# P's pass without the low half of h in its first block of channels, and the diagonals on GpSimd

## The chip, the cores and the metric

One core of a Trainium2 chip runs the kernel. The metric is the time of one execution on the device in microseconds (us); smaller is better. The time given is the median of three runs.

## The reference

There are 128 graphs of 128 nodes with 512 channels each, one adjacency matrix of 128 x 128 for all, and two layers.

```python
h = relu(layernorm(x))
z_l = h @ W_lang.T;  z_g = h @ W_grav.T;  v = h @ W_V.T
zn  = z_l / max(norm(z_l), eps)
A_l = max(zn @ zn.T, 0) * not_eye                     # cosine similarities
d2  = max(sq + sq.T - 2 * z_g @ z_g.T, 0)             # sq: squared norms of z_g
A_g = exp(-d2 / (2 * sigma**2)) * not_eye
K   = w_l * row_normalised(A_l * adj) + (1 - w_l) * row_normalised(A_g * adj)
x   = x + (K @ v) @ W_O.T
h2  = relu(layernorm(x))
x   = x + (adj * adj).T @ h2 + bias
```

W_lang has been scaled up by 8. Everything is float32.

## The kernel before

**Form of the computation.** The kernel never forms z_l and z_g. It takes M = W.T W once (for each of the two, l = 0 and 1) and needs S = h M h.T. M is symmetric, so only its blocks on and below the diagonal are kept (`Lw`, the ten blocks of `TRI`, those on the diagonal halved). With y the product of this half and h, P = y h.T is half of the result, and S = P + P.T. The values are float32 split into two parts of a shorter type, hi and lo, and a product is three matmuls (`passes`): hi·hi, hi·lo, lo·hi. Low parts are made as value minus hi, the hi part on ScalarE, the subtraction mostly on VectorE.

**Tiling and loops.** 32 groups of four graphs each (`NG`, `GB`). Each engine has a program of its own with a loop over the groups (`iteration(i)`), written out by hand; within an engine the order is that of the code, and semaphores with counts tie engines together. Iterations 0, 1, the last but one and the last stand outside of the loop. PSUM has a ring of five banks: use n may start when `drained` says that use n - 5 has been emptied (`free`).

**One iteration i on TensorE** (from `iteration` in the tensor block): eight y blocks (four blocks of channels a, l = 0 and 1), 60 matmuls of 512 columns; P's pass (line 1109), for each a and each graph b three matmuls of 256 columns, 48 in all, into `p_ps`; v of the first graph, 12 matmuls; K·v of group i - 1, 12 matmuls (waits for `kt_split`); v of the other three graphs, 36; layer 1 of group i - 2, 12. The y blocks of the next iteration wait for all four `ht_lo`.

**P to S.** ScalarE copies P out of PSUM in two halves (line 530, `p_copied`). VectorE multiplies each half by `select`, a repeated mask `diag_of` that keeps two diagonals (line 900, `diagonal`), reduces them to squared norms (line 907, `squares`), and clips them (line 911). GpSimd raises them to the power -1/2 (line 404, `row_norms`). P is turned by a transpose in blocks on VectorE (line 878, `turn_p`, once for each l), a store to DRAM, and eight loads back in turned order on SyncE's queue (lines 251 and 256). In the next iteration VectorE adds P and its turned copy (line 884, `sum_s`), ScalarE takes the exponential, and mask, row sums and factors follow on VectorE. VectorE then forms K (line 730, `combine`, `k_ready`) and K is turned in the same way: transpose (line 737), a store (line 281), four loads (line 286), then the copy `KT_hi` (line 610) on ScalarE and the subtraction `KT_lo` (line 746, `kt_lo`, gives `kt_split`) on VectorE. The buffer of the diagonals also holds the blocked P and K on their way out.

**VectorE around the change**, in order: the eight `y_lo` (line 669) with the work on S and K between them, the block transposes of the next group's h (line 685), four `bn_stats` (line 680), first diagonal, `KT_lo`, squares, second diagonal, squares, `v_lo(0)`, the clip, residual adds (line 750) with statistics, then low parts of v and of the next group's turned h (line 689, hT_lo) with the two `turn_p`, and last four outputs (line 780).

**GpSimd**, in order: four subtractions `h2_lo` (line 398), then behind a wait for `kt_split` two adds of the bias to rows of x (line 383), the row norms, two more such adds, the factors of both layer norms (lines 361 to 375), and the multiplication of spread norms and mask (line 389).

Of the kernel before, what the change touches and what calls it, by code (L numbers as in the profile page):

```python
# [20 lines left out]
def gnn_pair(nc, x, adj, w_lang, w_grav, w_v, w_o, gate_logit, log_sigma, bias, out):  # L21
# [34 lines left out]
    with ExitStack() as ctx:  # L56
        def sb(name, shape, dt=F32):
            return ctx.enter_context(nc.sbuf_tensor(name, shape, dt))
# [9 lines left out]
        Lw = [sb(f"Lw_{s}", [P, 2, len(TRI), P], F32R) for s in ("hi", "lo")]  # L68
        MT = [sb(f"MT_{s}", [P, C, D], F32R) for s in ("hi", "lo")]
# [7 lines left out]
        adj_sb = sb("adj_sb", [P, P])  # L77
# [4 lines left out]
        adj2 = sb("adj2", [P, P])  # L82
# [55 lines left out]
        def bank(use):  # L138
            return ring[:, use % BANKS]
# [89 lines left out]
        spread = y_rows[0][:, 1, 0:P]  # L229

# [115 lines left out]
        def _(pool):  # L346
# [61 lines left out]
            def iteration(i, before=True, lag=True, after=True, x_next=True):  # L408
                if lag:
                    for b in range(GB):  # L410
                        h2_lo(i - 2, b)

                    pool.wait_ge(kt_split, i)
                    add_bias(i - 2, 0)
                    add_bias(i - 2, 1)
                row_norms(i)
                if lag:
                    add_bias(i - 2, 2)
                    add_bias(i - 2, 3)
# [42 lines left out]
        def _(act):  # L462
            act.dma_start(gate, gate_logit.unsqueeze(0).to_broadcast([P, 1])).then_inc(consts_loaded, 16)
            act.dma_start(lsig, log_sigma.unsqueeze(0).to_broadcast([P, 1])).then_inc(consts_loaded, 16)
            act.dma_start(adj_sb[:, :], adj).then_inc(consts_loaded, 16)
# [158 lines left out]
            def lw_hi(l, banks, done, c0=0, c1=C):  # L624
                for c in range(c0, c1):
                    act.wait_ge(setup_mm, C * l + c + 1)
                    for a in range(c, C):
                        e = act.activation(Lw[0][:, l, blk[a, c]], banks[c][:, (a - c) * P:(a - c + 1) * P],
                                           ACT.Copy, scale=0.5 if a == c else 1.0)
                    e.then_inc(done, 1)  # L630
# [16 lines left out]
            act.activation(A2[0][:, :], adj2[:, :], ACT.Copy).then_inc(a2_hi, 1)  # L647
# [14 lines left out]
        def _(dve):  # L662
            def part(t):
                return t.bitcast(F32)
# [128 lines left out]
            def iteration(i, before=True, lag=True, after=True, x_next=True):  # L793
# [38 lines left out]
                if before:  # L832
                    diagonal(i, 0)
                    kt_lo(i - 1)
                    squares(i, 0)
                    diagonal(i, 1)
                    squares(i, 1)
                    v_lo(0)
# [52 lines left out]
            select = diag_of[:, :, :].rearrange("p l m -> p (l m)").unsqueeze(1).to_broadcast([P, GB // 2, 2 * P])  # L891

            def diagonal(g, q):
                half = slice(q * GB // 2, (q + 1) * GB // 2)
                if q == 0:
                    wait_for(dve, rn_step, RN_STEPS * g)
                    wait_for(dve, p_shifted, g)
                    wait_for(dve, k_stored, 16 * g)
                dve.wait_ge(p_copied, 2 * g + q + 1)
                dve.tensor_tensor(diag[:, half].rearrange("p b l m -> p b (l m)"),  # L900
                                  P_sb[:, half].rearrange("p b l m -> p b (l m)"), select, ALU.mult)\
                   .then_inc(diag_ready, 1)

            def squares(g, q):
                half = slice(q * GB // 2, (q + 1) * GB // 2)
                dve.wait_ge(diag_ready, 2 * g + q + 1)
                dve.tensor_reduce(sq[:, half], diag[:, half], AX.X, ALU.add).then_inc(sq_ready, 1)
# [5 lines left out]
            def squared_norms(g):  # L913
                for q in range(2):
                    diagonal(g, q)
                    squares(g, q)
                clipped_squares(g)

            def last_chain(i, n, use, hi):
# [3 lines left out]
                diagonal(i, 0)  # L923
                kt_lo(i - 1)
                squares(i, 0)
                diagonal(i, 1)
# [61 lines left out]
            dve.tensor_tensor(mask[:, :], adj_sb[:, :], off_diag[:, :], ALU.mult)  # L988
            dve.tensor_tensor(adj2[:, :], adj_sb[:, :], adj_sb[:, :], ALU.mult).then_inc(a2_step, 1)
# [17 lines left out]
            dve.tensor_tensor(A2[1][:, :], adj2[:, :], part(A2[0][:, :]), ALU.subtract).then_inc(a2_step, 1)  # L1007
# [18 lines left out]
        def _(pe):  # L1026
# [16 lines left out]
            def y_block(a, l, n, use):  # L1043

                free(use)
                product(bank(n), [t for c in range(a + 1) for t in passes(
                    [w[:, l, blk[a, c]] for w in Lw],
                    [w[:, c].rearrange("p b m -> p (b m)") for w in hT])]).then_inc(g_done, 1)
# [39 lines left out]
            def iteration(i, before=True, lag=True, after=True):  # L1088
# [138 lines left out]
```

## Time and profile before

| | |
|---|---|
| time, median of 3 runs | 1214.26 us (1213.69 to 1215.14) |
| profiled execution | 1213.74 us, span 1212.0 us |
| TensorE matmul | 1190.9 us busy, 98% of the span |
| VectorE | 1120.8 us, 92% |
| ScalarE | 707.0 us, 58% |
| GpSimd | 609.5 us, 50% |
| DMA | 160 GB/s on the mean |

The span is the time from the first to the last instruction of the profiled execution; its time has a little around that. Busy means that an instruction is in the engine. Matmuls overlap in the records, so their cost is read from the chain of work that ended last or from the distance between starts. VectorE's operations overlap as well, by some 0.1 us: one of 128x512 is listed with 0.69 and followed by the next after 0.6. The granted TensorE clock is at full speed (1.00) throughout the even part of the span.

### The profile page before, as it was taken

The numbers are of one execution on the slowest core, as the hardware profiler recorded it, in microseconds if no ns is written. First come the engines' busy times: TensorE is split into PE (matmuls) and PEld (weight loads), VectorE is DVE, ScalarE is ACT, GpSimd is POOL, SyncE is SP. The second block draws the span as 40 slices with busy tenths as digits, with TensorE's granted clock in tenths as the row PEclk, the third lists the DMA queues.
The fourth block names the chain that finished last, engine by engine and source line by source line (L and its number), as shares of the span: only waits on it lengthen the run. The fifth ranks groups of instructions, "written<-read, shape, count | busy, mean of one in ns | idle before, by whom it ended". The sixth has DMA issues, their size and how long they took to land.

```text
span 1212.0 us, 22868 instructions
## 1 busy us (share of the span) xinstructions
PE 1190.9 (98%) x5968; PEld 1009.5 (83%) x5968; DVE 1120.8 (92%) x1919; ACT 707.0 (58%) x1326; POOL 609.5 (50%) x988
## 2 busy tenths in 40 slices
PE   7999999999999999999999999999999999999996
PEld 6887888888888888888888888888888888888884
DVE  6678999999999999999999999999999999999878
ACT  5355556666556666555656555666655566655544
POOL 2103655545565555565454566554556545546543
PEclk9999999999999999999999999999999999999998
DMA  7333555554554564555565455555455556445412
GB/s 258 100 120 90 166 161 166 190 176 154 170 168 149 178 193 154 165 165 157 168 194 170 150 175 163 157 181 188 152 170 165 151 169 199 159 158 159 136 48 104
DMA packets 182416, 193.85 MB, mean 160 GB/s; under 512 B 20352, under 2 KB 131584, under 8 KB 182400
## 3 DMA queue, kind: packets, MB, share of 16 engines
q1 hardware_dynamic: 181824, 193.33, 51.2%
q10 hardware_dynamic: 576, 0.33, 0.1%
q8 instruction: 7, 0.11, 0.0%
q14 instruction: 9, 0.07, 0.0%
HBM read 103.09 MB, written 90.50 MB: 160 GB/s over the span
## 4 chain that ended last, share of the span: by engine, by line
PE 94%; DVE 3%; ACT 1%; DMA 1%; issue 1%; SPq 1%; POOL 0%; ACTq 0%; DVEq 0%
PE ring L1040 50%; PE ring L1131 27%; PE p_ps L1109 15%; PE ring L1158 1%; DVE x_ring L750 0%; DMA x_ring<-in_L_gnn_W_lang 0%; SPq L256 0%; DVE chain L900 0%; ACT h L481 0%; PE ring L1167 0%; DMA h<-p_dram 0%; DVE deg L716 0%; SPq L286 0%; DVE K L730 0%; DVE hT_lo L669 0%
## 5 line engine op out<-in xcount | busy, mean ns | idle before, releaser
L398 POOL TENSOR_TENSOR h_lo<-h2f,h_hi 128x512 fp32r<-128x512 f32 x124 | 157.1, 1298 | 301.7 <-ACT h_hi L584 301.6
L1040 PE MATMUL ring<-hT_hi,Lw_hi 128*128 128x512 f32 x640 | 249.4, 390 | 4.2 <-DVE hT_lo L689 1.5
L1040 PE MATMUL ring<-hT_hi,Lw_lo 128*128 128x512 f32 x640 | 249.0, 389 | 0.0
L1040 PE MATMUL ring<-hT_lo,Lw_hi 128*128 128x512 f32 x640 | 249.0, 389 | 0.0
L502 ACT ACTIVATE y_hi<-ring 128x512 fp32r<-128x512 f32 x256 | 148.5, 592 | 111.8 <-PE ring L1040 109.0
L552 ACT ACTIVATE v_hi<-ring 128x512 fp32r<-128x512 f32 x128 | 76.4, 598 | 227.5 <-PE ring L1131 158.8
L1131 PE MATMUL ring<-MT_hi,hT_hi 128*128 128x512 f32 x512 | 203.0, 397 | 0.3 <-DVE v_lo L669 0.3
L1131 PE MATMUL ring<-MT_lo,hT_hi 128*128 128x512 f32 x512 | 199.9, 390 | 0.0
L1131 PE MATMUL ring<-MT_hi,hT_lo 128*128 128x512 f32 x512 | 199.5, 390 | 0.0
L383 POOL TENSOR_TENSOR x_ring<-x_ring,bias_sb 128x512 f32 (+1 forms) x120 | 166.2, 1406 | 48.1 <-DVE KT_lo L746 48.1
L669 DVE TENSOR_TENSOR y_lo<-ring,y_hi 128x512 fp32r<-128x512 f32 x256 | 166.9, 681 | 19.6 <-ACT y_hi L502 19.6
L1040 PEld LDWEIGHTS ring<-hT_hi,Lw_hi 128*128 128x128 f32 x640 | 120.1, 188 | 30.0 <-issue 3.8
L1109 PE MATMUL p_ps<-y_hi,hT_lo 128*128 128x256 f32 x512 | 144.9, 283 | 0.0
L1109 PE MATMUL p_ps<-y_lo,hT_hi 128*128 128x256 f32 x512 | 144.9, 283 | 0.0
L1109 PE MATMUL p_ps<-y_hi,hT_hi 128*128 128x256 f32 x512 | 144.7, 283 | 0.0
L1040 PEld LDWEIGHTS ring<-hT_hi,Lw_lo 128*128 128x128 f32 x640 | 120.1, 188 | 25.1
L1040 PEld LDWEIGHTS ring<-hT_lo,Lw_hi 128*128 128x128 f32 x640 | 120.2, 188 | 24.8
L1131 PEld LDWEIGHTS ring<-MT_hi,hT_hi 128*128 128x128 f32 x512 | 96.2, 188 | 27.4 <-DVE v_lo L669 9.0
L1131 PEld LDWEIGHTS ring<-MT_hi,hT_lo 128*128 128x128 f32 x512 | 96.2, 188 | 20.7
L1131 PEld LDWEIGHTS ring<-MT_lo,hT_hi 128*128 128x128 f32 x512 | 96.3, 188 | 18.0
L575 ACT ACTIVATE h2f<-x_ring,ln 128x512 f32 (+1 forms) x128 | 97.1, 805 | 5.9 <-POOL ln L375 5.9
L1109 PEld LDWEIGHTS p_ps<-y_lo,hT_hi 128*128 128x128 f32 x512 | 98.2, 192 | 1.2
(187 smaller groups left out, 2503.1 us busy)
## 6 DMA issues: line engine op xcount, KB each, us to landing
x_ring<-in_x SPq DMA_DIRECT2D x32, 1024.0 KB, 5.3
out<-x_ring SPq DMA_DIRECT2D x128, 256.0 KB, 2.5
h_dram<-h SPq DMA_DIRECT2D x62, 512.0 KB, 3.4
h_turned<-h_dram SPq DMA_DIRECT2D x248, 128.0 KB, 3.3
p_dram<-chain SPq DMA_DIRECT2D x62, 256.0 KB, 2.1
h<-p_dram SPq DMA_DIRECT2D x248, 64.0 KB, 2.6
rn_cols<-rn_dram SPq DMA_DIRECT2D x31, 256.0 KB, 3.9
k_dram<-chain SPq DMA_DIRECT2D x31, 256.0 KB, 2.0
```

The source lines that it names most:

```text
L383: pool.tensor_tensor(x_rows(g, b), x_rows(g, b), bias_sb[:, :], ALU.add).then_inc(x2b_ready, 1)
L398: pool.tensor_tensor(h2[1][:, b], h2f[:, b], h2[0][:, b].bitcast(F32), ALU.subtract)\
L502: act.activation(y[0][:, a, :, l], bank(n).rearrange("p (b m) -> p b m", b=GB), ACT.Copy)\
L552: act.activation(v[0][:, b], bank(n + v_use(b, before)), ACT.Copy).then_inc(hi_ready, 1)
L575: act.activation(h2f[:, b], x_rows(g, b), ACT.Relu, bias=ln[:, SHIFT, b:b + 1], scale=ln[:, RSTD, b:b + 1]).then_inc(h2_done, 1)
L669: return dve.tensor_tensor(out, ps, part(hi), ALU.subtract)
L1040: mm = pe.matmul(out, lhsT, rhs, start=(k == 0), stop=(k == len(terms) - 1))
L1109: mm = pe.matmul(p_ps[:, b].rearrange("p l m -> p (l m)"), lhsT, rhs, start=(a == 0 and k == 0 and b % 2 == 0), stop=(a == C - 1 and k == ...
L1131: mm = pe.matmul(bank(m), lhsT, rhs, start=(c == 0 and k == 0), stop=(c == C - 1 and k == len(terms) - 1))
L1158: mm = pe.matmul(bank(c)[:, 0:D - c * P], lhsT, rhs, start=(e == 0 and k == 0), stop=(e == C - 1 and k == 2))
```

## The change

1. P's pass leaves out the product of h's low part and y's high part in the first block of channels (a = 0), 4 of 48 matmuls. In exchange y_block(0) multiplies the low part of h by the diagonal block of M unhalved (`M0`, a new tile, written by ScalarE in the setup). Since S = P + P.T, the term that one side misses is doubled on the other.
2. The two diagonals of an iteration are made by GpSimd, behind a wait for `kt_split` (only in the last iteration by VectorE, as before). The waits for `rn_step` and `p_shifted` stay with VectorE, in `squares`.
3. On GpSimd the first two bias adds move from behind the `kt_split` wait to the front of the iteration, behind a wait for `k_ready`.
4. VectorE's order becomes: `KT_lo`, squares(0), `v_lo(0)`, squares(1), clip, adds.
5. `adj_sb` and `adj2` lie in the memory of A.

```diff
+        M0 = sb("M0", [P, 2, P], F32R)
...
-        adj_sb = sb("adj_sb", [P, P])
+        adj_sb, adj2 = chain[:, 2, 0, 0], chain[:, 2, 0, 1]
...
+        def diagonal(eng, g, q):
+            half = slice(q * GB // 2, (q + 1) * GB // 2)
+            if q == 0:
+                wait_for(eng, k_stored, 16 * g)
+            eng.wait_ge(p_copied, 2 * g + q + 1)
+            eng.tensor_tensor(diag[:, half].rearrange("p b l m -> p b (l m)"),
+                              P_sb[:, half].rearrange("p b l m -> p b (l m)"), select, ALU.mult)\
+               .then_inc(diag_ready, 1)
...
             def iteration(i, before=True, lag=True, after=True, x_next=True):
                 if lag:
+                    pool.wait_ge(k_ready, i)
+                    add_bias(i - 2, 0)
+                    add_bias(i - 2, 1)
                     for b in range(GB):
                         h2_lo(i - 2, b)
-
-                    pool.wait_ge(kt_split, i)
-                    add_bias(i - 2, 0)
-                    add_bias(i - 2, 1)
+                if after:
+                    if before:
+                        pool.wait_ge(kt_split, i)
+                    for q in range(2):
+                        diagonal(pool, i, q)
                 row_norms(i)
...
+                    if c == 0:
+                        act.activation(M0[:, l], banks[c][:, 0:P], ACT.Copy)
...
                 if before:
-                    diagonal(i, 0)
                     kt_lo(i - 1)
                     squares(i, 0)
-                    diagonal(i, 1)
+                    v_lo(0)
                     squares(i, 1)
-                    v_lo(0)
                     clipped_squares(i)
...
+                if a == 0:
+                    terms[1] = (M0[:, l], terms[1][1])
+                product(bank(n), terms).then_inc(g_done, 1)
...
                         terms = passes([w[:, a, b] for w in hT], [w[:, a, b].rearrange("p l m -> p (l m)") for w in y])
+                        terms = terms[:2] if a == 0 else terms
```

## Rows read from the trace of the kernel before

**Rows 1.** The page: busy us, share of the span and instructions of each engine.
```profile
PE 1190.9 (98%) x5968; PEld 1009.5 (83%) x5968; DVE 1120.8 (92%) x1919; ACT 707.0 (58%) x1326; POOL 609.5 (50%) x988
```

**Rows 2.** Chain that ended last, in order of time: start us, us, what.
```profile
140.30 16.32 PE ring L1040 x72
156.62 5.75 PE p_ps L1109 x48
...
165.12 2.72 PE ring L1040 x12
...
1145.02 16.32 PE ring L1040 x72
```

**Rows 3.** Timeline of VectorE and TensorE: start us, us, instruction, [idle before].
```profile
557.13 1.06 DVE L900 TENSOR_TENSOR chain<-chain,diag_of 128x512 f32<-128x512 f32 x1
...
561.69 0.68 DVE L669 TENSOR_TENSOR v_lo<-ring,v_hi 128x512 fp32r<-128x512 f32 x1
...
562.42 0.50 PE L1131 MATMUL ring<-MT_hi,hT_hi 128*128 128x512 f32 x1
562.76 0.39 PE L1131 MATMUL ring<-MT_lo,hT_hi 128*128 128x512 f32 x1
...
631.24 1.58 DVE L900 TENSOR_TENSOR chain<-chain,diag_of 128x512 f32<-128x512 f32 x1
```

**Rows 4.** Timeline of VectorE and ScalarE over one iteration.
```profile
605.82 0.70 DVE L878 STREAM_TRANSPOSE chain<-chain 128x512 f32<-128x512 f32 x1
...
613.52 2.01 DVE L884 TENSOR_TENSOR chain<-h,chain 128x512 f32<-128x512 f32 x2
...
622.23 0.71 DVE L737 STREAM_TRANSPOSE chain<-K 128x512 f32<-128x512 f32 x1
...
629.38 0.62 ACT L610 ACTIVATE KT_hi<-K 128x512 fp32r<-128x512 f32 x1
630.04 0.69 DVE L746 TENSOR_TENSOR KT_lo<-K,KT_hi 128x512 fp32r<-128x512 f32 x1
...
634.13 1.28 DVE L750 TENSOR_TENSOR x_ring<-ring,x_ring 128x512 f32 x2
...
641.71 0.70 DVE L878 STREAM_TRANSPOSE chain<-chain 128x512 f32<-128x512 f32 x1
...
644.10 0.68 DVE L689 TENSOR_TENSOR hT_lo<-h_turned,hT_hi 128x512 fp32r<-128x512 f32 x1
```

**Rows 5.** Last loads of turned P and K: issue ns, when, us to landing.
```profile
L256 SPq DMA_DIRECT2D h<-p_dram x2: 432/432/432, 610.3 to 610.7; - x2
DMA to landing us min/median/max: 2.7/2.7/2.8
...
L286 SPq DMA_DIRECT2D K<-k_dram x1: 432/432/432, 626.9 to 626.9; - x1
DMA to landing us min/median/max: 1.9/1.9/1.9
```

**Rows 6.** The diagonals: their group (busy us, mean ns), and the first in the timeline.
```profile
L900 DVE TENSOR_TENSOR chain<-chain,diag_of 128x512 f32<-128x512 f32 x64 | 82.5, 1289 | 9.6 <-ACT chain L530 9.4
...
47.87 0.69 DVE L900 TENSOR_TENSOR chain<-chain,diag_of 128x512 f32<-128x512 f32 x1 [0.71 <-ACT chain L530]
```

**Rows 7.** Timeline of GpSimd.
```profile
541.16 1.58 POOL L389 TENSOR_TENSOR chain<-rn_cols,mask 128x512 f32<-128x512 f32 x1 [1.57 <-DMA rn_cols<-rn_dram]
552.57 5.07 POOL L398 TENSOR_TENSOR h_lo<-h2f,h_hi 128x512 fp32r<-128x512 f32 x4 [9.83 <-ACT h_hi L584]
...
563.78 2.54 POOL L383 TENSOR_TENSOR x_ring<-x_ring,bias_sb 128x512 f32 x2
...
630.98 3.01 POOL L383 TENSOR_TENSOR x_ring<-x_ring,bias_sb 128x512 f32 x2 [1.58 <-DVE KT_lo L746]
```

**Rows 8.** Chain that ended last: from a GpSimd subtraction to the matmul behind it.
```profile
1196.71 0.14 issue
```

**Rows 9.** Timeline of VectorE in the last iteration: its second diagonal.
```profile
1169.49 1.41 DVE L900 TENSOR_TENSOR chain<-chain,diag_of 128x512 f32<-128x512 f32 x1
```

More of the change, by code:

```diff
@@ L81, in gnn_pair @@
         mask = sb("mask", [P, P])
-        adj2 = sb("adj2", [P, P])
         A2 = [sb(f"A2_{s}", [P, P], F32R) for s in ("hi", "lo")]
@@ L229, in gnn_pair @@
         spread = y_rows[0][:, 1, 0:P]
+        select = diag_of[:, :, :].rearrange("p l m -> p (l m)").unsqueeze(1).to_broadcast([P, GB // 2, 2 * P])
+        def diagonal(eng, g, q):
[6 more added lines that the diff above has]
+               .then_inc(diag_ready, 1)
         block = ctx.enter_context(nc.Block())
@@ L464, in _ @@
             act.dma_start(lsig, log_sigma.unsqueeze(0).to_broadcast([P, 1])).then_inc(consts_loaded, 16)
-            act.dma_start(adj_sb[:, :], adj).then_inc(consts_loaded, 16)
+            act.dma_start(adj_sb, adj).then_inc(consts_loaded, 16)
             act.dma_start(bias_sb[:, :], bias.unsqueeze(0).to_broadcast([P, D])).then_inc(consts_loaded, 16)
@@ L646, in _ @@
             act.wait_ge(a2_step, 1)
-            act.activation(A2[0][:, :], adj2[:, :], ACT.Copy).then_inc(a2_hi, 1)
+            act.activation(A2[0][:, :], adj2, ACT.Copy).then_inc(a2_hi, 1)
             for q in range(C):
@@ L889, in sum_s_last, with squares @@
                 dve.tensor_tensor(A, p_ps[:, :, :, :], P_sb, ALU.add).then_inc(s_ready, 2)
-            select = diag_of[:, :, :].rearrange("p l m -> p (l m)").unsqueeze(1).to_broadcast([P, GB // 2, 2 * P])
-            def diagonal(g, q):
+            def squares(g, q):
                 half = slice(q * GB // 2, (q + 1) * GB // 2)
@@ L897, in diagonal @@
                     wait_for(dve, p_shifted, g)
[L898 to L905, printed above, removed]
                 dve.wait_ge(diag_ready, 2 * g + q + 1)
@@ L914, in squared_norms @@
                 for q in range(2):
-                    diagonal(g, q)
                     squares(g, q)
@@ L921, in v_lo @@
                     lo(v[1][:, b], bank(n + v_use(b, True)), v[0][:, b], hi + b + 1).then_inc(drained, 1)
-                diagonal(i, 0)
+                diagonal(dve, i, 0)
                 kt_lo(i - 1)
                 squares(i, 0)
-                diagonal(i, 1)
+                diagonal(dve, i, 1)
                 squares(i, 1)
@@ L987, in _ @@
             dve.wait_ge(consts_loaded, 16 * 4)
-            dve.tensor_tensor(mask[:, :], adj_sb[:, :], off_diag[:, :], ALU.mult)
-            dve.tensor_tensor(adj2[:, :], adj_sb[:, :], adj_sb[:, :], ALU.mult).then_inc(a2_step, 1)
+            dve.tensor_tensor(mask[:, :], adj_sb, off_diag[:, :], ALU.mult)
+            dve.tensor_tensor(adj2, adj_sb, adj_sb, ALU.mult).then_inc(a2_step, 1)
             dve.wait_ge(exp_gate, 2)
@@ L1006, in _ @@
             dve.wait_ge(a2_hi, 1)
-            dve.tensor_tensor(A2[1][:, :], adj2[:, :], part(A2[0][:, :]), ALU.subtract).then_inc(a2_step, 1)
+            dve.tensor_tensor(A2[1][:, :], adj2, part(A2[0][:, :]), ALU.subtract).then_inc(a2_step, 1)
             iteration(0, before=False, lag=False)
@@ L1045, in y_block @@
                 free(use)
-                product(bank(n), [t for c in range(a + 1) for t in passes(
+                terms = [t for c in range(a + 1) for t in passes(
                     [w[:, l, blk[a, c]] for w in Lw],
-                    [w[:, c].rearrange("p b m -> p (b m)") for w in hT])]).then_inc(g_done, 1)
+                    [w[:, c].rearrange("p b m -> p (b m)") for w in hT])]
+                if a == 0:
+                    terms[1] = (M0[:, l], terms[1][1])
+                product(bank(n), terms).then_inc(g_done, 1)
             def transposes_K_last(g):
```

## Prediction

> **What bounds the kernel now.** I read the page's busy shares first [rows 1]: TensorE is busy for 98% of the span, VectorE for 92%, and GpSimd for 50%. The chain that ended last gives the shape [rows 2]: one iteration is a run of 72 matmuls (layer 1 of an earlier group and the y blocks, 16.32 us), the 48 of P's pass (5.75), 12 of v, 12 of K·v, 36 of v. The same piece of 72 begins at 140.30 and, 28 iterations on, at 1145.02, so the period is 1004.72 / 28 = 35.88 us. A matmul of P costs 5.75 / 48 = 0.120 us on this chain, one of 512 columns 2.72 / 12 = 0.227.
>
> TensorE isn't bound by its own work alone. Behind K·v its next matmul starts at 562.42, just as v_lo(0) ends on VectorE (561.69 + 0.68), and the one after at 562.76: a step of 0.34 in place of 0.227, so 0.11 us lost per iteration [rows 3]. And VectorE at 92% has almost no holes. So before I believe in a saving on TensorE I look for a ring of dependences that closes over one iteration, as such a ring has a period of its own. One runs through two DMA round trips. Taken from 606.5 to 642.4 us [rows 4, 5]:
> - the second transpose of P (line 878) ends at 605.82 + 0.70 = 606.52; the last load of turned P is issued at 610.7 and lands 2.8 later, when the sum S (line 884) starts, 613.52: 7.0 us
> - from there to the end of K's transpose (622.23 + 0.71 = 622.94): 9.4
> - K to DRAM and back, last load issued at 626.9, landing 1.9 later: 628.8: 5.9
> - KT_hi could start then; it starts at 629.38, takes 0.62, and KT_lo starts at 630.04: 0.7 of work and 0.5 of slack
> - from KT_lo to the first residual add (line 750, 634.13): 4.1
> - from there, VectorE back to back, to the end of the second transpose of P (641.71 + 0.70 = 642.41): 8.3
>
> Without the slack that is 35.4 us. TensorE binds, but the ring is only 0.5 us behind it.
>
> **The change part by part.** (1) P's pass loses one of three products in the first of four channel blocks: 4 matmuls of 0.120, 0.48 us per iteration, all on the chain. y_block(0) multiplies h_lo by the unscaled M0 in place of the halved block: as many matmuls of the same shapes, cost nothing.
>
> (2) The two diagonals (line 900) leave VectorE. Their mean there is 1289 ns, but alone, with GpSimd idle, one takes 0.69 (at 47.87) [rows 6]; the rest is waiting for GpSimd, as in the 1.58 us at 631.24 [rows 3] with a pair of bias adds from 630.98 beside it [rows 7]. VectorE is relieved of 2.6 us an iteration. But it needs the results itself, and now they come from an engine that is slower and must first be told.
>
> (3) On GpSimd the first diagonal waits for kt_split, the end of KT_lo; behind it on that engine's queue are the second diagonal, the row norms, two bias adds and the norms of the next layer. Today two bias adds wait so: KT_lo ends at 630.04 + 0.69 = 630.73 and they start at 630.98, 0.25 later [rows 4, 7]; the new order has about as many waits behind that one, so 0.25 again. No diagonal ran on GpSimd. The nearest rows are the bias adds, both operands contiguous, 2.54 / 2 = 1.27 each undisturbed, and the mask multiplication (line 389), 1.58, with a repeated operand like the diagonal's and another read with a stride, which the diagonal's isn't [rows 7]. I take 1.27; the range is 1.27 to 1.58. The way back from GpSimd to VectorE isn't seen; GpSimd to TensorE took 0.14 [rows 8]. I take 0.09, between that and nothing.
>
> With D for the start of the first diagonal: it ends at D + 1.27, squares(0) starts at D + 1.36, and v_lo(0), now behind it, at D + 1.96 (steps of 0.6, as between 630.04 and 634.13 without the diagonal), ending at D + 2.6. The second diagonal ends at D + 2.54, squares(1) starts at D + 2.63. The clip waits for its result, 0.7 later, as v_lo(0) no longer stands between them, and the add follows at D + 3.4. From KT_lo to the add that is 0.69 + 0.25 + 3.4 = 4.35 against 4.1 now. The relief is spent waiting, and the ring is 0.25 to 0.3 longer: 35.65.
>
> (4) Two bias adds move ahead of the four h_lo subtractions and wait for k_ready. K is there just before its transpose starts, 622.1 to 622.2 [rows 4]; with 0.25 and six operations of 1.27, GpSimd is through at 630.0. In the ring KT_lo would start at 628.8 + 0.7 = 629.5, while the last subtraction runs. What that does is seen at 557.13: a diagonal started there takes 1.06, ending 0.55 behind the last of the subtractions beside it (552.57 + 5.07 = 557.64) [rows 3, 7]. So KT_lo would end at 630.5 and not at 630.2: up to 0.3 more. Where the loads of K land later it is nothing; I take 0.1. For the consumers of h_lo, a layer later, a microsecond more or less is free.
>
> The Trainium skill says why ("SBUF — State Buffer", section "SBUF: two separate sides"): GpSimd and a VectorE operation with two SBUF inputs share a port pair under an exclusive lock, held for a whole instruction. The rows agree (1.58 and 1.06 against 0.69). From this "Perfetto Trace Analysis" of the Trainium skill, section "Optimizing Scalar/DVE Operations", warns that moving work between those two engines might not help; rival D is the form that this would take here.
>
> The ring then has 35.75 us, TensorE alone 35.88 − 0.48 − 0.11 = 35.29 (v_lo(0) would no longer end behind K·v). The ring takes over and leaves 0.13 to 0.15 us per iteration, 28 × 0.15 = 4.2. What is late next is the fourth hT_lo (line 689, 644.10 + 0.68), which stands a fixed 2.4 us behind the second transpose of P [rows 4]: TensorE would wait for it some 0.45 us ahead of each first y block.
>
> (5) Outside the even stretch, P's passes of iterations 0, 1 and the last save 3 × 0.48 = 1.4. In the last iteration the diagonals stay on VectorE and the bias adds beside the second go: 1.41 to 0.69, 0.7 [rows 9]. The ring is longer in iterations 1 and 2 as well: 2 × 0.3 lost. Two extra ScalarE copies in the setup: an estimated 0.2 lost. Sum 1.3 gained. That adj and adj2 lie in A's memory costs nothing, as A is first written an iteration after they were read; nor do squares' moved waits, for what is an iteration old.
>
> **Sum.** Span 1212.0 − 4.2 − 1.3 = 1206.5; with the 1.7 us between span and time of the profiled execution (1213.74), 1208.2; that execution lies 0.5 under the median of the runs. Forecast: 1209.
>
> **The rivals.** A: TensorE stays the bound. The ring is a sum of single rows, with DMA landings that vary by some tenths and handovers that I have guessed. If it comes out 0.5 shorter, the period is 35.29 and the gain 28 × 0.59 + 1.9 (the ends without the ring's loss) = 18 to 19: 1195. Against it: nothing in the rows makes the ring that much shorter.
>
> B: the ring takes back all. If KT_lo always waits the whole 0.3 for the last subtraction, the period is 35.95, or 35.9 with quick handovers, and only the ends' gain remains: 1213. The port rows speak for it; against it, the landings of K would always have to be early.
>
> C, slower: the diagonals cost what the mask multiplication costs, 1.58 each, since both have a repeated operand. They lie end to end in the ring: 0.62 more, 36.37, 28 × 0.49 − 1.3 = 12.4 slower: 1226. It decides from about 1.35 us a diagonal on. Against it: the stride of the other operand, which the two don't share.
>
> D, slower by the port: GpSimd is through with the subtractions 0.3 later than computed (adds of 1.3, started 0.4 behind K), and KT_lo ends 0.4 later than in my sum: 36.1, 28 × 0.22 − 1.3 = 5 slower: 1219.
>
> That the change doesn't do what it says has no weight of its own: 128 matmuls go in any case; whether they are worth something is B.
>
> **How the numbers follow.** Forecast (its own spread 1203 to 1211.8) 0.48; A 0.12; B 0.22; C 0.11; D 0.07. About 0.2% (2.4 us) is what a measurement of this kernel can tell from no change: faster 0.60, same 0.22, slower 0.18. The range takes in A and D and leaves out C and the edges: 1195 to 1219.
>
> **What would show it.** P's stretch of the chain at 5.27 us. Diagonals on GpSimd at 1.27 (C: 1.5 and more). VectorE idle some 1.5 us ahead of squares(0), released by GpSimd. KT_lo at up to 1 us in place of 0.69 where a subtraction runs (B, D). TensorE waiting for hT_lo (line 689) about 0.4 us ahead of the y blocks, once per iteration; without that wait the period will be near 35.3, and A holds. A period of 35.75 on the chain. I am wrong if the wait sits elsewhere, for instance at kt_split ahead of K·v, or if S starts earlier than 7.0 us behind P's transpose.

## The result, and the profile after

| | before | after |
|---|---|---|
| time, median of 5 runs | 1215.14 us (1213.69 to 1215.18) | 1219.74 us (1219.64 to 1221.44) |
| ratio after / before | | 1.0047 (1.0035 to 1.0059) |
| profiled execution: time, span | 1213.74, 1212.0 us | 1221.44, 1219.7 us |

The change makes the kernel slower by 0.5%; 1209 us had been forecast, and 1219.74 lies outside of the range of 1195 to 1219. (The median before is over five runs here; over three it was 1214.26.)

The profiled execution of after is the slowest of its five runs, 1.7 above their median, and that of before is 1.4 below its own. The spans therefore differ by 7.7 us and the medians by 4.6, and a difference per iteration that is read from the two traces can be too large by up to (7.7 − 4.6) / 30 = 0.1 us.

The page of after. First the busy shares (us, share of the span, instructions), then the chain that ended last, by engine and by line:
```profile
PE 1183.9 (97%) x5840; PEld 993.8 (81%) x5840; DVE 1056.3 (87%) x1857; ACT 710.1 (58%) x1328; POOL 674.2 (55%) x1050
...
PE 36%; DVE 25%; DMA 12%; issue 10%; SPq 9%; ACT 5%; POOL 2%; DVEq 1%; ACTq 0%; POOLq 0%
```
TensorE has 128 matmuls fewer and VectorE 64 us less work than in [rows 1], and the span is longer all the same. In the kernel before, the chain was one run of matmuls after another [rows 2]. Now TensorE has 36% of it, and the rest is spread over VectorE, the DMA and its issue. Over half of these 36% lies behind 888 us, where the chain steps back from the fourth hT_lo to a wait (DVEq L801) that stands behind it on VectorE's queue, and so to TensorE. In the timeline that hT_lo follows the v_lo before it without a gap (1009.06, 1009.66), so this part of the chain isn't a cause, and I go by the periods and the sums below. The same chain in order of time, one iteration of it (start us, us, what):
```profile
574.05 0.63 DVE chain L897
...
578.88 2.85 DMA h<-p_dram
581.75 1.16 DVE chain L903
...
590.20 0.72 DVE chain L758
590.94 2.02 DMA k_dram<-chain
...
594.86 2.18 DMA K<-k_dram
597.12 0.64 ACT KT_hi L629
597.78 0.74 DVE KT_lo L767
598.78 1.29 POOL chain L240
600.15 0.30 issue
600.70 0.68 DVE v_lo L690
601.38 0.67 DVE sq L916
602.66 0.30 issue
602.96 0.69 DVE x_ring L771
```
That is the ring of the prediction: P's transpose, the P trip, S, K, the K trip, KT_hi, KT_lo, GpSimd's first diagonal (L240), the squares, the residual adds. It has almost no slack left: in 23 of 27 iterations KT_hi starts 0.08 behind the landing of K (here 594.86 + 2.18 = 597.04), where it started 0.5 behind it before [rows 4, 5].

The period can be read without the chain, from KT_hi, which runs once per iteration. Its row of after (min/median/max ns, first and last start us):
```profile
L629 ACT ACTIVATE KT_hi<-K x31: 624/632/636, 90.8 to 1174.4; 128x512 fp32r<-128x512 f32 x31
```
(1174.4 − 90.8) / 30 = 36.12 us; the same row of before (L610) goes from 91.4 to 1167.6, 35.87. The 30 periods are 7.4 of the 7.7 us between the spans; the start is 0.6 shorter, the tail 0.9 longer.

The waits (engine, what, for what: us in total, times, longest):
```profile
DVE sq L916 <- POOL chain L240: 49.4, 32, 1.7
...
DVE KT_lo L767 <- ACT KT_hi L629: 29.3, 30, 3.1
...
PE ring L1048 <- DVE hT_lo L710: 15.4, 29, 1.8
```
TensorE stands 0.5 us an iteration ahead of the first y block, for the fourth hT_lo. VectorE stands about 1.55 us per iteration for GpSimd's diagonal, and 1 us for KT_hi.

The ring by the steps of the prediction, in us, means over 27 iterations of the even stretch, worked out from the starts and ends in each timeline. "Trip of P" is from the end of the second P transpose to the last landing; "S, K" from there, with any wait, to the end of K's transpose; "trip of K" to its last landing; then the wait for KT_hi's start, KT_hi to KT_lo's start, KT_lo to the first residual add, and the add to the next second P transpose.

| kernel | trip of P | S, K | trip of K | wait | KT_hi | KT_lo to add | add to P | sum |
|---|---|---|---|---|---|---|---|---|
| before | 7.02 | 9.33 | 5.97 | 0.54 | 0.66 | 4.08 | 8.28 | 35.89 |
| forecast | 7.0 | 9.4 | 5.9 | 0 | 0.7 | 4.45 | 8.3 | 35.75 |
| after | 7.05 | 9.33 | 6.01 | 0.10 | 0.66 | 4.69 | 8.29 | 36.14 |

(The forecast's 4.45 is 4.35 and the 0.1 for the port.) The one step that grew by more than 0.04 is KT_lo to add, by 0.61 where 0.37 had been forecast.

### The profile page after: what moved, and what is told of

Its sections match the earlier page's. It is cut to its first block, busy times and chain, and to the rows that moved or that the text cites. A ratio compares the mean times of both kernels' runs of the same rounds, so it can differ in the third digit from the quotient of the medians.

```text
span 1219.7 us, 22642 instructions
## 1 busy us (share of the span) xinstructions
PE 1183.9 (97%) x5840; PEld 993.8 (81%) x5840; DVE 1056.3 (87%) x1857; ACT 710.1 (58%) x1328; POOL 674.2 (55%) x1050
## 4 chain that ended last, share of the span: by engine, by line
PE 36%; DVE 25%; DMA 12%; issue 10%; SPq 9%; ACT 5%; POOL 2%; DVEq 1%; ACTq 0%; POOLq 0%
PE ring L1048 20%; PE ring L1144 10%; PE p_ps L1122 5%; SPq L269 4%; DMA h<-p_dram 4%; DMA K<-k_dram 3%; DMA k_dram<-chain 3%; SPq L299 3%; DVE x_ring L771 3%; DVE v_lo L690 2%; DVE bn L774 2%; DVE deg L737 2%; DVE chain L903 2%; POOL chain L240 2%; DVE K L751 2%
## 5 line engine op out<-in xcount | busy, mean ns | idle before, releaser
L396 POOL TENSOR_TENSOR x_ring<-x_ring,bias_sb 128x512 f32 (+1 forms) x120 | 153.1, 1297 | 241.2 <-DVE K L751 241.2
L1048 PE MATMUL ring<-hT_hi,Lw_hi 128*128 128x512 f32 x640 | 253.0, 395 | 18.0 <-DVE hT_lo L710 15.4
L1048 PE MATMUL ring<-hT_lo,Lw_hi 128*128 128x512 f32 x576 | 224.6, 390 | 0.0
L1144 PE MATMUL ring<-MT_hi,hT_hi 128*128 128x512 f32 x512 | 200.3, 391 | 0.0
L1122 PE MATMUL p_ps<-y_lo,hT_hi 128*128 128x256 f32 x512 | 139.4, 283 | 0.0
L1122 PE MATMUL p_ps<-y_hi,hT_hi 128*128 128x256 f32 x512 | 139.2, 283 | 0.0
L1048 PEld LDWEIGHTS ring<-hT_lo,Lw_hi 128*128 128x128 f32 x576 | 108.4, 188 | 22.8
L240 POOL TENSOR_TENSOR chain<-chain,diag_of 128x512 f32<-128x512 f32 x62 | 78.8, 1293 | 61.2 <-DVE KT_lo L767 41.6
L1122 PE MATMUL p_ps<-y_hi,hT_lo 128*128 128x256 f32 x384 | 108.7, 283 | 0.0
```

Source lines behind the costliest of these rows:

```text
L240: eng.tensor_tensor(diag[:, half].rearrange("p b l m -> p b (l m)"), P_sb[:, half].rearrange("p b l m -> p b (l m)"), select, ALU.mult)\
L396: pool.tensor_tensor(x_rows(g, b), x_rows(g, b), bias_sb[:, :], ALU.add).then_inc(x2b_ready, 1)
L1048: mm = pe.matmul(out, lhsT, rhs, start=(k == 0), stop=(k == len(terms) - 1))
L1122: mm = pe.matmul(p_ps[:, b].rearrange("p l m -> p (l m)"), lhsT, rhs, start=(a == 0 and k == 0 and b % 2 == 0), stop=(a == C - 1 and k == ...
L1144: mm = pe.matmul(bank(m), lhsT, rhs, start=(c == 0 and k == 0), stop=(c == C - 1 and k == len(terms) - 1))
```

## The experiments

In all of them the question is which ring or engine sets the period, and what each part of the change is worth. The period is taken from KT_hi's row each time, (last − first start) / 30.

### The parts of the change, one by one

Three parts can be switched separately: the trimmed P pass (with M0), the early bias adds, the diagonals on GpSimd. Five kernels fill the table below.

e1_tensor_only: the trimmed pass alone; both diagonals on VectorE and the bias adds behind `kt_split`, as before.
```diff
+                if a == 0:
+                    terms[1] = (M0[:, l], terms[1][1])
...
+                        terms = terms[:2] if a == 0 else terms
```


> The changed kernel with GpSimd's and VectorE's order put back as before: only the trimmed P pass and M0 stay. Theory RING (a ring of dependences through the two DMA round trips, in which the way from KT_lo to the first residual add lies, sets the period): the ring of before has 35.4 us, TensorE alone 35.3, so the period goes from 35.88 to about 35.4 and the time to 1199 to 1203. Theory TENSOR (the trimmed matmuls or M0 are worth nothing or cost something by themselves): 1213 or more, no change against before. Theory PORT (the moved bias adds alone make the change slow): as RING here, it doesn't tell the two apart.

1209.74 us, ratio 0.9954 (0.9937 to 0.997). Period (1162.4 − 90.2) / 30 = 35.74. The gain is less than half of what was expected (1199 to 1203).

e2_tensor_bias: the same with the early bias adds.
```diff
+                    pool.wait_ge(k_ready, i)
+                    add_bias(i - 2, 0)
+                    add_bias(i - 2, 1)
                     for b in range(GB):
                         h2_lo(i - 2, b)
-                    pool.wait_ge(kt_split, i)
-                    add_bias(i - 2, 0)
-                    add_bias(i - 2, 1)
```


> As the previous kernel, and in addition the two bias adds ahead of the h_lo subtractions, behind k_ready, as in the changed kernel; the diagonals stay on VectorE. Theory RING: the second diagonal no longer has a bias add beside it (1.57 to 0.69 us), the way from KT_lo to the first add falls from 4.08 to 3.2, the ring to 34.5, TensorE binds at 35.3: 1195 to 1198, faster than both kernels. Theory PORT: the early bias adds and late subtractions hold up VectorE, so this is slower than the kernel with the adds in their old place, and near 1215 or above.

1201.68 us, ratio 0.9882 (0.9862 to 0.9903), period (1155.5 − 91.3) / 30 = 35.47. It is the fastest kernel of the study, ahead of both before and after: the change without its move of the diagonals. It is still 4 us above what was expected (1195 to 1198).

e3_gpsimd_only: the changed kernel with the complete P pass.
```diff
-                if a == 0:
-                    terms[1] = (M0[:, l], terms[1][1])
...
-                        terms = terms[:2] if a == 0 else terms
```


> The changed kernel with all three products in P's pass again (and M0 not used): only the moves between VectorE and GpSimd. Theory RING: TensorE alone has 35.8 us and the ring 36.14, so the 0.48 us of matmuls per iteration come back out of idle time: period 36.1 to 36.2, time 1220 to 1223, only 1 to 3 us above the changed kernel. If TensorE still set the time, it would be 15 us above it: 1235.

1227.38 us, ratio 1.0099 (1.0082 to 1.0115), period (1179.6 − 91.3) / 30 = 36.28. That is 7.6 above the changed kernel, where 1 to 3 had been expected. The matmuls don't come out of idle time alone, as ScalarE shows:
```profile
562.09 1.32 ACT L549 ACTIVATE chain<-p_ps 128x512 f32<-128x512 f32 x2 [0.94 <-PE p_ps L1118]
563.31 0.62 ACT L629 ACTIVATE KT_hi<-K 128x512 fp32r<-128x512 f32 x1
```
K has landed at 562.72, but ScalarE copies P out ahead of KT_hi and waits for P's pass to do it. In 20 of 27 iterations KT_hi starts right behind this copy, in after in 6 of 28. So there is a second ring, which the prediction didn't have: y blocks, P's pass, the copy of P, KT_hi, KT_lo, the diagonals, the adds, the fourth hT_lo, and the next y blocks. In e3 it takes 36.17 us (y blocks start at 543.12 and 579.29); without the 0.48 of matmuls that makes an estimated 35.69 for after, where the ring with the DMA trips is longer most of the time.

e4_bias_back: the changed kernel with the first two bias adds back, behind the diagonals.
```diff
-                    pool.wait_ge(k_ready, i)
-                    add_bias(i - 2, 0)
-                    add_bias(i - 2, 1)
...
+                if lag:
+                    add_bias(i - 2, 0)
+                    add_bias(i - 2, 1)
```


> The changed kernel with the two bias adds behind the two diagonals on GpSimd in place of ahead of the h_lo subtractions. Theory RING: KT_lo goes from a mean of about 0.85 us to 0.69, no other term of the ring changes, the period falls by 0.16 and the time to 1214 to 1217. Theory PORT: the loss goes altogether, 1208 or less. If neither, 1220.

1236.12 us, ratio 1.0163 (1.0145 to 1.018), period (1190.3 − 91.7) / 30 = 36.62. This was far off: 1214 to 1217 had been expected, and it is the slowest of the five.

e12_bias_only: the kernel before with the early bias adds alone.

> The kernel before with the early bias additions alone: P's pass is complete again, the diagonals are on VectorE, and GpSimd adds the first two biases ahead of the h_lo subtractions. Theory (TensorE's own work, 35.9 us an iteration, is the bound of the kernel before, with the ring 0.5 us shorter; the bias additions let the diagonals start earlier, so that only TensorE's stall of 0.11 us ahead of f1's first block can go): period 35.75 to 35.9, 1209 to 1215 us, so most of the 13.5 us that the two parts bring together needs the trimmed pass. Rival (the early biases hold up VectorE through the shared port): over 1217 us. Rival (the order on GpSimd alone brings it): under 1206 us.

1207.94 us, ratio 0.9944 (0.9928 to 0.9961), period (1162.8 − 92.0) / 30 = 35.69; the time is 1 us below the expected 1209 to 1215. The expectation rested on a stall of 0.11 us ahead of the second v block [rows 3]; over 29 iterations of before it is 0.16 on the mean.

Together (us, and the ratio to before; each set of runs had runs of before beside it):

| | P pass complete | P pass trimmed |
|---|---|---|
| diagonals on VectorE, late bias adds | 1214 to 1216 (before) | 1209.7 (0.9954) |
| diagonals on VectorE, early bias adds | 1207.9 (0.9944) | 1201.7 (0.9882) |
| diagonals on GpSimd, early bias adds | 1227.4 (1.0099) | 1219.7 (1.0047) |
| diagonals on GpSimd, late bias adds | | 1236.1 (1.0163) |

Along each row the trimmed pass brings about 6 to 8 us, the early bias adds bring 7 to 9 (16 once the diagonals are on GpSimd), and the diagonals on GpSimd cost 18 to 20 with the early adds and 26 with the late ones (which stand behind the diagonals there). The change is a gain of 14 us and a loss of 18 to 20.

The rings of the first four kernels, as above:

| kernel | trip of P | S, K | trip of K | wait | KT_hi | KT_lo to add | add to P | sum |
|---|---|---|---|---|---|---|---|---|
| e1 | 7.10 | 9.32 | 6.07 | 0.11 | 0.79 | 4.07 | 8.28 | 35.75 |
| e2 | 7.16 | 9.33 | 6.02 | 0.24 | 1.28 | 3.18 | 8.28 | 35.50 |
| e3 | 7.16 | 9.31 | 6.04 | 0.25 | 0.66 | 4.57 | 8.29 | 36.29 |
| e4 | 7.16 | 9.34 | 6.07 | 0.09 | 0.66 | 4.68 | 8.64 | 36.65 |

Between e2 and after only the diagonals differ. They put 1.51 us into KT_lo to add and take 0.62 out of KT_hi to KT_lo; 0.25 less of waits and late landings leaves 0.64 an iteration, 19 us of the 18 to 20.

What each row rests on. In e12 the whole chain between 140 and 1150 us is TensorE's (shares by line):
```profile
by line: PE ring L1045 53.8%; PE ring L1137 30.3%; PE p_ps L1115 15.9%
```
TensorE alone thus needs 35.69 with the complete pass, and without 4 × 0.120 35.21; the prediction had 35.29. The stall ahead of the second v block [rows 3] is gone there too: with the early adds no bias add runs beside the second diagonal. In e1 both diagonals are held, the first by the h_lo subtractions, the second by the late bias adds. Timelines of e1, VectorE, GpSimd and TensorE:
```profile
590.30 1.35 DVE L240 TENSOR_TENSOR chain<-chain,diag_of 128x512 f32<-128x512 f32 x1
...
592.77 1.57 DVE L240 TENSOR_TENSOR chain<-chain,diag_of 128x512 f32<-128x512 f32 x1
...
594.98 0.68 DVE L683 TENSOR_TENSOR v_lo<-ring,v_hi 128x512 fp32r<-128x512 f32 x1
```
```profile
587.29 3.81 POOL L411 TENSOR_TENSOR h_lo<-h2f,h_hi 128x512 fp32r<-128x512 f32 x3
```
```profile
595.15 0.39 PE L1044 MATMUL ring<-v_hi,KT_lo 128*128 128x512 f32 x1
595.72 0.50 PE L1140 MATMUL ring<-MT_hi,hT_hi 128*128 128x512 f32 x1 [0.18 <-DVE v_lo L683]
```
The step of 0.57 in place of 0.227 is a stall of 0.34, and the step behind it (595.72 to 596.05) has 0.11 more. In before these are 0.02 and 0.11 [rows 3], on the mean of 29 iterations 0.16 together, against 0.47 here. v_lo(0) didn't come earlier with the matmuls that went, so TensorE waits for it, and 0.31 of the 0.48 is gone at once.

In e2 only the first diagonal is held. Its VectorE and GpSimd:
```profile
550.98 1.78 DVE L240 TENSOR_TENSOR chain<-chain,diag_of 128x512 f32<-128x512 f32 x1
552.69 0.68 DVE L761 TENSOR_TENSOR KT_lo<-K,KT_hi 128x512 fp32r<-128x512 f32 x1
...
553.89 0.68 DVE L240 TENSOR_TENSOR chain<-chain,diag_of 128x512 f32<-128x512 f32 x1
...
555.80 0.16 DVE L916 TENSOR_SCALAR sqc<-sq 128x4 f32<-128x4 f32 x1
555.87 1.28 DVE L765 TENSOR_TENSOR x_ring<-ring,x_ring 128x512 f32 x2
```
```profile
547.13 5.09 POOL L411 TENSOR_TENSOR h_lo<-h2f,h_hi 128x512 fp32r<-128x512 f32 x4
```
The first diagonal ends at 552.76, 0.54 behind GpSimd's subtractions (552.22), the same distance as in [rows 3, 7]. It costs the ring only 0.6 (KT_hi to KT_lo 1.28 against 0.66), because most of it lies in the time that K is under way. The second takes 0.68, and from KT_lo to the add 3.18 us pass against 4.69 in after. The expectation had this step right (3.2), but had nothing for the held first diagonal, so its ring of 34.5 is 1.0 short, 0.6 of it from there.

In e4 the adds stand behind the diagonals, and what runs beside them is hT_lo(0) and the clip. VectorE of e4:
```profile
573.20 0.52 DVE L919 TENSOR_SCALAR sqc<-sq 128x4 f32<-128x4 f32 x1
573.64 1.28 DVE L770 TENSOR_TENSOR x_ring<-ring,x_ring 128x512 f32 x2
...
578.24 1.02 DVE L709 TENSOR_TENSOR hT_lo<-h_turned,hT_hi 128x512 fp32r<-128x512 f32 x1
```
The clip takes 0.52 in place of 0.17, hT_lo(0) 1.02 in place of 0.67, both with a GpSimd add beside them. The step from the add to P's transpose is 8.64 against 8.29. What I had counted as a relief of KT_lo (its mean is 0.69 here) came back twice elsewhere. The rest of the 0.51 by which the sum exceeds that of after lies in the two trips (7.16 and 6.07).

### Is it the ring?

If a ring with two trips sets the period, lengthening or shortening a trip must move it. SyncE's queue issues the spread of the norms (`rn_cols`) among P's loads; moved behind the last of P's loads, P lands earlier.
```diff
                 fetch_p(g, 0)
+                fetch_p(g, 1)
                 sp.wait_ge(rn_stored, 16 * g + 16)
                 sp.dma_start(rn_cols[:, :, :], rn_dram.unsqueeze(0).to_broadcast([P, P, GB])).then_inc(rn_spread, 16)
-                fetch_p(g, 1)
```
The edit is the same in three kernels: the changed one (e5_norms_last), e2 (e7_both_norms_last) and the one before (e8_before_norms_last).

> The changed kernel with one DMA moved on SyncE's queue: the spread of the norms is issued behind the last four loads of turned P in place of ahead of them. Theory RING: P's way from its second transpose to S gets 0.3 to 0.45 us shorter, and the sum S no longer has the mask multiplication of GpSimd beside it (up to 0.5 us), so the ring falls from 36.14 to 35.4 or less; a second ring then binds, that runs through the y blocks, P's pass, KT_hi, KT_lo, the diagonals and the fourth hT_lo, with 35.7: 1207 to 1211. If the DMA trips are not on the way that sets the time: 1220, no change against the changed kernel.

> The kernel with the trimmed P pass, the early bias adds and the diagonals on VectorE (1201.7), and the spread of the norms issued behind the loads of turned P. Theory RING: with the DMA way 0.3 us or more shorter, the iterations in which late loads of K hold TensorE up (mean period 35.5, undisturbed 35.3) go away: 1195 to 1199. If that kernel is bound by TensorE alone, no change: 1201.

> The kernel before with only that DMA moved on SyncE's queue. Theory RING: TensorE binds there, with 0.5 us between it and the ring, so a shorter ring is worth nothing: 1213 to 1216. If it gets faster by more than 3 us, the DMA trip already bound the kernel before, and my reading of its slack was wrong.

1252.72 us (1.0307), 1230.94 (1.013) and 1233.95 (1.0156): slower, all three. P did land 0.9 to 1.2 earlier (trips of 6.06, 6.01, 6.08), but S needs the norms too, and these, issued last, now land later than P. VectorE and GpSimd of e5:
```profile
632.81 1.28 DVE L903 TENSOR_TENSOR chain<-h,chain 128x512 f32<-128x512 f32 x2
636.15 0.69 DVE L718 SCALAR_TENSOR_TENSOR chain<-chain 128x512 f32<-128x512 f32 x1 [2.06 <-POOL chain L402]
```
```profile
634.46 1.57 POOL L402 TENSOR_TENSOR chain<-rn_cols,mask 128x512 f32<-128x512 f32 x1 [3.59 <-DMA rn_cols<-rn_dram]
```
The masking of the language half (L718) stands 2.06 us for GpSimd's mask multiplication, which needs the spread norms. I had taken a later line for the first reader of them. As tests of the ring they serve after all, with the sign turned. In all three, P's transpose to K's transpose now takes 17.4 to 17.5 us, 1.0 more than in their parents (16.36 in before). In the changed kernel, whose ring has no slack, the sum goes from 36.14 to 37.14, all of it. In the kernel before it goes from 35.89 to 36.52: the first 0.4 to 0.5 vanish in the slack, the rest is paid, although TensorE has exactly the same work.

### Taking single steps out of the changed ring

e6_no_kt_wait: GpSimd's diagonals no longer wait for `kt_split`.
```diff
-                    if before:
-                        pool.wait_ge(kt_split, i)
```


> The changed kernel without GpSimd's wait for kt_split ahead of the diagonals (what they read and write is guarded by other waits). The first diagonal then starts right behind the h_lo subtractions and overlaps KT_lo. Theory RING: KT_lo is held up by the port to the end of a diagonal, but the diagonals come 0.9 us earlier and squares(1) about 0.6: period near 35.6, time 1206 to 1212. A theory that only the port contention of KT_lo counts says slower: KT_lo at 1.5 to 1.9 us, K.v on TensorE later, 1225 or more.

1219.42 us, ratio 1.0033 (1.0016 to 1.005), not to be told from the changed kernel by time, where 1206 to 1212 had been expected. The ten runs spread from 1215.5 to 1225.4, more than any other kernel's, and the profiled one (1216.66) is below their median; period (1170.6 − 90.3) / 30 = 36.01, KT_lo to add 4.47. VectorE:
```profile
561.00 0.77 DVE L765 TENSOR_TENSOR KT_lo<-K,KT_hi 128x512 fp32r<-128x512 f32 x1 [0.93 <-ACT KT_hi L627]
562.94 0.69 DVE L914 TENSOR_REDUCE sq<-chain 128x4 f32<-128x512 f32 x1 [1.18 <-POOL chain L240]
563.88 0.69 DVE L688 TENSOR_TENSOR v_lo<-ring,v_hi 128x512 fp32r<-128x512 f32 x1 [0.25 <-ACT v_hi L569]
```
The first squares come 1.94 behind KT_lo's start and no longer 2.3, but v_lo(0) behind it now waits for v_hi, a product of TensorE: the next thing is late at once.

e9_first_half_early, and e10_both_first_half_early, the same edit on e2: the first half of S added before P has landed completely.
```diff
-                act.wait_ge(s_ready, 2 * g + (2 if isinstance(g, int) and g == NG - 1 else 1))
+                act.wait_ge(s_ready, 2 * g + 2)
...
+                        if before and n == 2:
+                            sum_s(i - 1, 0)
                         if before and n == 3:
                             sum_s(i - 1, 1)
-                            sum_s(i - 1, 0)
```


> The changed kernel with one order on VectorE altered: the sum that makes the first half of S is taken up ahead of the third y_lo subtraction and no longer behind the last one, as soon as P has landed, so that one of the two sums that stood between the landing and the exponential is out of the loop through P, S and K. Theory (that loop, 36.14 us an iteration in the changed kernel, sets its period): the segment from the landing to S's transpose end becomes 0.5 to 0.85 us shorter, and the period goes to about 35.7 us, where a loop through TensorE's own next blocks takes over; 1206 to 1211 us. Rival (the period is set elsewhere, by TensorE or by GpSimd): the period stays at 36.1 us, 1218 to 1222 us.

> The fastest kernel so far (TensorE's part with the two early bias additions, diagonals on VectorE, 1201.7 us) with the same alteration of VectorE's order. There the loop takes 35.5 us an iteration, and its shortest iterations 35.2 to 35.3. Theory (late landings of K are what lifts half of the iterations above the floor): with 0.5 to 0.85 us of slack in the loop the landings' scatter is absorbed and the mean falls to 35.3 us, 1195 to 1199 us. Rival (TensorE's own work is already the bound there): no change, 1200 to 1203 us.

1225.9 us (1.0094, 1.0078 to 1.0111) and 1207.57 (0.9944, 0.9928 to 0.9961): both about 6 us slower than their parents, periods (1179.8 − 91.3) / 30 = 36.28 and (1159.7 − 90.3) / 30 = 35.65. VectorE and GpSimd of e9:
```profile
583.04 0.68 DVE L904 TENSOR_TENSOR chain<-h,chain 128x512 f32<-128x512 f32 x1
...
584.24 1.47 DVE L904 TENSOR_TENSOR chain<-h,chain 128x512 f32<-128x512 f32 x1
```
```profile
583.25 1.90 POOL L402 TENSOR_TENSOR chain<-rn_cols,mask 128x512 f32<-128x512 f32 x1 [1.24 <-DMA rn_cols<-rn_dram]
```
The half that ScalarE's exponential needs (`sum_s(., 1)`) already stood first, and the other lay beside the exponential, so nothing left the ring. What the edit did is put an addition (583.04) beside the start of GpSimd's mask multiplication (583.25): that takes 1.90 in place of 1.56, ends at 585.15, and the addition that the exponential waits for ends 0.56 behind it. "S, K" is 9.51 against 9.33. So the ring grew by 0.18 us and the time by 6.2 / 28 = 0.22 per iteration. In e10 "S, K" grew by 0.28 (9.61 against 9.33), the wait ahead of KT_hi fell from 0.24 to 0.08, and the sum rose by 0.19; the time rose by 5.9 / 28 = 0.21. Both fit the ring: about a fifth of a microsecond put into it costs about as much as it says.

e11_clip_later: the clip behind the first two adds.
```diff
-                    clipped_squares(i)
                     add(i - 1, 0, n + 1)
                     add(i - 1, 1, n + 2)
+                    clipped_squares(i)
```


> The changed kernel with the clip of f1 moved from ahead of the two additions behind KT_lo to behind them; the squares, the diagonals on GpSimd and the bias additions stay. Theory (the additions stand in the loop, and the clip with the issue behind it costs 0.3 to 0.45 us there): the segment from KT_lo to the first addition falls from 4.69 to about 4.3 us, period 35.8, 1209 to 1214 us. Rival (the additions are not late for anyone, TensorE is busy with other blocks then): within 1 us of 1219.7. Against: hT_lo comes later for TensorE by as much as the clip is, which would show as a longer stall ahead of y.

1224.42 us, ratio 1.0078 (1.0061 to 1.0095), period (1178.5 − 91.0) / 30 = 36.25. VectorE and GpSimd:
```profile
572.26 1.19 DVE L710 TENSOR_TENSOR hT_lo<-h_turned,hT_hi 128x512 fp32r<-128x512 f32 x1
```
```profile
570.35 2.55 POOL L396 TENSOR_TENSOR x_ring<-x_ring,bias_sb 128x512 f32 x2
```
KT_lo to add fell to 4.31, 0.38 less, as expected for a clip in the ring; the time that was expected with it (1209 to 1214) did not come. For GpSimd's row norms wait for the clip, so its next two bias adds start later and hold hT_lo(0): 1.19 in place of 0.67, and the add to P's transpose takes 8.80 in place of 8.29. In after these adds are over just before hT_lo(0).

## Why the prediction was wrong

The step that failed is the sum of the ring with the DMA trips, put at 35.75 us, just under the 35.88 of before; it measures 36.14. The mechanism (the ring takes over from TensorE) was right. The term most mis-sized is the way from KT_lo to the add, 4.45 forecast and 4.69 measured.

**What bounds the kernel before: right.** TensorE sets the period and the ring is 0.5 behind. TensorE alone came out at 35.69 (e12), and the ring showed itself when it was made longer (e8). Its stall was read from one iteration as 0.11 and is 0.16 on the mean, so TensorE alone after the change is 35.21 and not 35.29; the second ring, through the copy of P, is missing from the prediction (e3).

**(1) The trimmed pass: right.** On the chain of after P's stretch of 44 matmuls (from 84.97) takes 5.27 us, where 5.75 stood.

**(2) and (3) The diagonals: the price right, the path behind them too short.** Their group in after (busy us, mean ns of one):
```profile
L240 POOL TENSOR_TENSOR chain<-chain,diag_of 128x512 f32<-128x512 f32 x62 | 78.8, 1293 | 61.2 <-DVE KT_lo L767 41.6 <-ACT chain L549 19.5
```
That is 1.27 each where two follow one another, not the 1.58 of rival C; they start 0.25 behind KT_lo's end, as forecast. The way back to VectorE is 0.03 us, less than the 0.09 that I took. The VectorE rows of after on which the failing step shows:
```profile
600.09 0.69 DVE L916 TENSOR_REDUCE sq<-chain 128x4 f32<-128x512 f32 x1 [1.58 <-POOL chain L240]
600.70 0.68 DVE L690 TENSOR_TENSOR v_lo<-ring,v_hi 128x512 fp32r<-128x512 f32 x1
601.34 0.69 DVE L916 TENSOR_REDUCE sq<-chain 128x4 f32<-128x512 f32 x1
602.06 0.17 DVE L920 TENSOR_SCALAR sqc<-sq 128x4 f32<-128x4 f32 x1
602.35 1.29 DVE L771 TENSOR_TENSOR x_ring<-ring,x_ring 128x512 f32 x2
```
With D = 598.76 (the timeline's start of the diagonal) the clip starts at D + 3.30, as forecast (3.33). The add was to follow at D + 3.4 and follows at D + 3.59: 0.29 behind the clip's start, where it is 0.07 in e2 (555.80, 555.87). The clip here is held by its own wait for squares(1), and the instructions on VectorE's queue between it and the add (register steps and the add's wait) are in the trace only once it has started (602.08 and 602.18, the clip at 602.06); in e2 they are at 555.33 and 555.44, ahead of the clip, while v_lo(0) runs. Mean over 27 iterations from the diagonal's start to the add: 3.58.

**(4) The early bias adds: the price somewhat low.** KT_lo takes 0.85 in the mean (median 0.867, least 0.691), 0.16 above its cost alone where I took 0.1. The rows' reading, a VectorE operation that ends 0.55 behind GpSimd's, held for every operation with two inputs. As the first table shows I never asked what these adds are worth by themselves: 7 to 8 us.

**The ring's sum, the step that failed: 0.39 us too short.** KT_lo to add has 0.24 of it (0.17 behind the diagonal, 0.06 in KT_lo). The other 0.14 lie in the segments that I had taken from one iteration and rounded: 0.05 more for P's trip and 0.11 for K's, and 0.10 from K's landing to KT_hi, less 0.12 in S, KT_hi and the rest. The means of before would already have given 0.02 of the first and 0.07 of the second. In the kernel before, the 0.5 of slack swallowed late landings; a ring without slack pays for each. That last sentence is an argument from the table, not a test of its own.

**(5) The ends: wrong by 1.7.** The even stretch has 28 × (36.14 − 35.88) = 7.3 of the 7.7 us between the spans, so the ends lost 0.4 where 1.3 were to be gained. The first KT_hi is 0.6 earlier, the tail behind the last 0.9 longer. Part of the tail is in VectorE's rows of the last iteration of after:
```profile
1173.51 1.54 DVE L240 TENSOR_TENSOR chain<-chain,diag_of 128x512 f32<-128x512 f32 x1 [3.48 <-ACT chain L549]
1175.07 1.69 DVE L767 TENSOR_TENSOR KT_lo<-K,KT_hi 128x512 fp32r<-128x512 f32 x1
```
The second diagonal did fall from 1.41 to 0.68, as forecast. But behind the early adds GpSimd's subtractions run until 1176.20 and hold the first diagonal (1.54, before 0.98) and KT_lo (1.69, before 0.69), which the prediction left out. KT_hi to the adds is 6.7 us against 6.4. The rest stays open. In both traces the granted clock is below 1.00 from about 12 us behind the last KT_hi on (0.84 to 0.93 before, 0.77 to 0.90 after, in stretches of 10 to 13 us).

One more thing differs in the profiled execution of after: TensorE stands for hT_lo until 105.70, then works, and from 107 to 110 us its granted clock is 0.50 (the lower level, 1.2 GHz). The stretch of 60 matmuls takes 15.51 us there and 13.9 elsewhere in that trace. e4 and e5 show the same, e3, e9 and e11 don't. How much of the 1.6 reaches the time isn't shown: the first period from KT_hi to KT_hi is 36.53 with it and 36.3 to 36.7 in those three without.

**What is late next: right.** TensorE waits for the fourth hT_lo ahead of y, 15.4 / 29 = 0.53 each.

**The rivals.** A needed a ring 0.5 shorter. B's price (KT_lo's whole 0.3) was half true. D gave 36.1 and 1219, which is the number measured, but for another reason: KT_lo was 0.06 later than in my sum, not 0.4. The trimmed pass and the early adds do what they say; the loss sits in the diagonals, since VectorE stands 1.55 us per iteration for work that takes it 0.68. The Trainium skill ("Perfetto Trace Analysis", section "Optimizing Scalar/DVE Operations") warns that offloading between the two engines might not help, and the runs agree: 1219.7 against 1201.7 us, 1.5% lost. Here, though, it isn't the shared port that takes the gain back but the dependence.

**The chances.** The forecast lived on a margin of 0.13 to 0.15 us an iteration between two sums of eight terms, each rounded to 0.1 or bounded by 0.1 to 0.3. Such a margin doesn't carry 0.60 for faster; terms that all err in one direction (waits that were left out are never negative) deserved more weight than two separate rivals of 0.11 and 0.07.

## What to carry to other kernels

Where a ring through a DMA round trip is within one or two per cent of the bound, cost each part of a change by what it puts into the ring, not by what it takes off a busy engine, and test the parts apart: here two of three were worth 14 us and the third lost more than that. An operation given to another engine whose result the first engine needs next turns its busy time into idle time, and the small instructions that used to hide behind full-size work come into view. In e4, e9 and e11 a reordering set a GpSimd operation beside another VectorE operation, and one of the two took up to 0.5 us longer: look which ones will meet, in the iteration's timeline, before moving it.

## What was not expected of the hardware

- An addition behind a tiny operation that was held by a wait starts 0.29 us behind that one's start (after), and 0.07 where full-size work ran ahead of it.
- A clip of 128x4, one input, is also held by a GpSimd add: 0.52 against 0.17 us (e4), ending 0.03 behind that add on the mean, where two-input operations of 128x512 end 0.54 to 0.56 behind.
- It goes both ways: GpSimd's mask multiplication took 1.90 with a VectorE addition beside its start (e9; 1.78 on the mean, against 1.57 in before).
- The handover from GpSimd to VectorE takes 0.03 us, the one from VectorE to GpSimd 0.25 (diagonals of after).
